# Dense graph layer: front and back products dealt in sixteen equal shares between the builds

## The reference, cut to what matters

```python
ew = _inv_sqrt(out_deg)[row] * w * _inv_sqrt(in_deg)[col]
mf = (x @ W_f.T)[row] * ew[:, None]
y_forward = jax.ops.segment_sum(mf, col, num_segments=n_nodes)
mb = (x @ W_b.T)[col] * ew[:, None]
y_backward = jax.ops.segment_sum(mb, row, num_segments=n_nodes)
y = jnp.concatenate([y_forward, y_backward], axis=-1) + bias_param
```

## Time and profile before

| | us |
|---|---|
| median of 3 runs | 5378.27 |
| lowest and highest run | 5376.85, 5378.61 |
| span of the profiled execution | 5371.9 |
| of it `gnn_dense`, from the first build to the last front sum | 3303.2 to 4639.3 |

### The profile page before, as it was taken

One profiled execution on the slowest core, in us unless ns is written; L12 is line 12 of the kernel. 1 busy time (PEld: TensorE's weight loads), 2 busy tenths in 40 slices (PEclk: granted clock), 3 DMA queues, 4 the chain that ended last, 5 costly groups with the idle time before them and its releaser, 6 DMA issues. The chain is left out here.

```text
span 5371.9 us, 86748 instructions
## 1 busy us (share of the span) xinstructions
PE 4172.9 (78%) x27330; PEld 3017.8 (56%) x27331; DVE 3413.4 (64%) x7289; ACT 1663.0 (31%) x2903; POOL 2167.4 (40%) x2194
## 2 busy tenths in 40 slices
PE   3477777777777777746999945999999999769992
PEld 2355555555555555534888833666656666458872
DVE  6466666666666666687555577888888888640115
ACT  1233333333333333321222264333333333121121
POOL 1477777777777777700666600000000000202220
PEclk9678777777777887756999966999999999759996
DMA  4766666666666666651566543444444444323333
GB/s 122 189 168 170 167 165 170 170 162 170 170 165 167 170 169 163 158 207 68 193 200 199 183 139 84 81 85 89 81 81 88 87 81 85 88 86 121 100 118 103
DMA packets 946866, 733.83 MB, mean 137 GB/s; under 512 B 703102, under 2 KB 832054, under 8 KB 944599
## 3 DMA queue, kind: packets, MB, share of 16 engines
q1 hardware_dynamic: 835851, 433.62, 31.3%
q0 software_dynamic: 104144, 289.95, 20.0%
q10 hardware_dynamic: 6652, 7.32, 0.4%
HBM read 483.39 MB, written 92.34 MB: 107 GB/s over the span
## 5 line engine op out<-in xcount | busy, mean ns | idle before, releaser
L1288 POOL DMA_INDIRECT gat_rows<-h_rows,gat_sources x1664 | 1577.0, 948 | 509.2 <-issue 485.5
L1526 PE MATMUL gat_sum_ps<-gat_rows,gat_onehot 128*128 128x265 f32 x3328 | 1167.6, 510 | 3.2 <-DVE gat_rows L1418 2.4
L1526 PEld LDWEIGHTS gat_sum_ps<-gat_rows,gat_onehot 128*128 128x128 f32 x3328 | 792.9, 250 | 190.4 <-issue 5.7
L2055 ACT CAST gnn_z<-build_ps 128x392 bf16<-128x392 f32 x992 | 473.4, 486 | 847.7 <-PE build_ps L2070 842.3
L1997 DVE TENSOR_TENSOR onehot_low<-dense_codes,dense_iota_bf 128x2048 bf16<-128x2048 bf16 x496 | 604.0, 1218 | 2.6 <-PE build_ps L2070 2.6
L2080 PE MATMUL back_ps<-zb_pieces,gnn_z 128*128 128x384 bf16 x3038 | 567.1, 327 | 0.0
L2102 PE MATMUL front_ps<-x_res_wide,front_rows 128*128 128x448 bf16 x2604 | 562.5, 353 | 0.0
L1976 POOL DMA_INDIRECT front_rows<-zf_piece_rows,vrow_nodes x62 | 64.8, 1046 | 1231.2 <-PE front_ps L2102 1221.0
L1418 DVE TENSOR_TENSOR gat_rows<-gat_rows,gat_numerators_ps 128x1024 f32<-128x1024 f32 x416 | 502.0, 1207 | 0.0
L2471 PE MATMUL moe_hidden_ps<-moe_rows_T,moe_w 128*128 128x256 f32 (+1 forms) x1408 | 459.9, 483 | 2.7 <-DVE moe_rows_T L2512 0.8
L2070 PEld LDWEIGHTS build_ps<-onehot_high,onehot_low 128*128 128x128 bf16 x7936 | 339.4, 98 | 204.6 <-issue 38.5
(11 more groups left out here) (366 smaller groups left out, 5160.4 us busy)
## 6 DMA issues: line engine op xcount, KB each, us to landing
moe_w<-in_L_ffn_W SPq DMA_DIRECT2D x112, 512.0 KB
gat_targets<-gat_step_targets SPq DMA_DIRECT2D x104, 512.0 KB
moe_w<-in_L_ffn_w SPq DMA_DIRECT2D x32, 1024.0 KB
gat_rows<-h_rows,gat_sources POOLq DMA_INDIRECT x1664
moe_rows_out<-moe_slot_zeros SPq DMA_DIRECT2D x36, 512.0 KB
gat_flags<-gat_tile_flags SPq DMA_DIRECT2D x104, 128.0 KB
normal_rows<-moe_xn_all SPq DMA_DIRECT2D x14, 896.0 KB
mid_taken<-moe_rows_out SPq DMA_DIRECT2D x14, 896.0 KB, 7.3
```

The lines of the kernel that those rows point to most:

```text
L1288: pool.indirect_dma_start(out=g[:, b, t, :], out_offset=None, in_=T.h[:, :], in_offset=bass.IndirectOffsetOnAxis(ap=idx[:, b, t:t + 1], ax ...
L1526: last = pe.matmul(po[:, s % BANKS, 0:W], o[:, b, s * SUB + t, :], g[:, b, s * SUB + t, :], start=t == 0, stop=t == SUB - 1)
L2055: nc.scalar.copy(AT[:, k % 2, :, CHUNK * c:CHUNK * (c + 1)], pb[:, c % 2, 0:CHUNK * NT].rearrange("p (u h) -> p h u", u=CHUNK)).then_inc(a ...
```

## The change

The front and back products of a slot are put in one list `run`: for each of seven groups first the 6 front products, then the 7 back products, 91 in all. The list is cut in sixteen shares of 5 or 6, and share c is issued behind the build of chunk c, now also in the chunks 0 and 15. `back_ps` has two banks, used in turn, so TensorE's wait for the sum of the superstep before the last (`q - 2` where it was `q - 1`) replaces that for the last one. The merge moves from chunk 1 to chunk 4. On VectorE the sums follow: a front sum stands four chunks behind the chunk in which its group ends (chunks 1, 3, 5, 7, 10, 12, 14), the sum of the back products behind chunk 15 and so at chunk 3 of the next slot, and the addition of the merged rows at chunk 8. The number of instructions of every kind stays the same.

```diff
+    TERMS = 6
+    MERGE = 4
+    run = [("front", g, n) if n < TERMS else ("back", g, n - TERMS) for g in range(GROUP) for n in range(TERMS + GROUP)]
+    share = [run[c * len(run) // NC:(c + 1) * len(run) // NC] for c in range(NC)]
+    front_done = [[g for kind, g, n in share[c] if kind == "front" and n == TERMS - 1] for c in range(NC)]
...
-        py = k.ps(ctx, "back_ps", [P, 512])
+        py = k.ps(ctx, "back_ps", [P, 2, 512])
...
             def sums(q, k, c):
-                if c == 1 and 2 <= k <= NQ + 1:
+                if c == MERGE and 2 <= k <= NQ + 1:
                     add_back(q, k)
-                if c % 2 and c <= 2 * HALF - 1 and 3 <= k <= NQ + 2:
-                    add_front(q, k, c)
-                if c == 2 * HALF and 1 <= k <= NQ:
+                if 3 <= k <= NQ + 2:
+                    for g in front_done[c]:
+                        add_front(q, k, g)
+                if c == NC - 1 and 1 <= k <= NQ:
                     sum_back(q, k)
...
-            def back(q, k, g):
-                if g == 0:
+            def back(q, k, g, n):
+                h = g * GROUP + n
+                if h == 0:
                     pe.wait_ge(ae, q * NC)
-                    until(pe, yr, q - 1)
...
+                    until(pe, yr, q - 2)
...
             def slot(q, r, k):
                 for c in range(NC):
                     if k < NQ:
                         build(q, k, c)
-                    if c % 2 == 0 and c and 1 <= k <= NQ:
-                        back(q, k, c // 2 - 1)
-                    if c == 1 and 2 <= k <= NQ + 1:
+                    for kind, g, n in share[c]:
+                        if kind == "front" and 3 <= k <= NQ + 2:
+                            front(q, r, k, g, n)
+                        if kind == "back" and 1 <= k <= NQ:
+                            back(q, k, g, n)
+                    if c == MERGE and 2 <= k <= NQ + 1:
                         merge(q, k)
-                    if c % 2 and c <= 2 * HALF - 1 and 3 <= k <= NQ + 2:
-                        front(q, r, k, c)
```

More of the change, by code:

```diff
@@ L1891, in gnn_dense @@
     HALF = PARTS // 2
+    TERMS = 6
[3 more added lines that the diff above has]
+    front_done = [[g for kind, g, n in share[c] if kind == "front" and n == TERMS - 1] for c in range(NC)]
+    assert HALF == GROUP
     io = k.sem("dense_iota")
@@ L1938, in supersteps, with front_at @@
                 slot(q, q // BODY, q)
-        def front_at(k, c):
+        def front_at(k, g):
             first = k % 2
-            return (c - 1) // 2 + (0 if first else HALF), (k - 3 if first else k - 4) % SLOTS
+            return g + (0 if first else HALF), (k - 3 if first else k - 4) % SLOTS
         @block.sync
@@ L2001, in onehots, with add_front @@
                 last.then_inc(oh, 1)
[L2003 to L2006, removed]
+            def add_front(q, k, g):
+                f = q * HALF + (g - 3 * HALF)
+                n = (k * HALF + g - 3 * HALF) % 2
+                at = front_at(k, g)[0] * CN
                 dve.wait_ge(yf, f + 1)
@@ L2015, in sum_back @@
                 dve.tensor_scalar(mrg[:, n, :], i2[:, :], C.vlocal[:, bass.ds(q - 1, 1)], None, ALU.is_equal)
-                dve.tensor_reduce(ybv[:, n, :], py[:, 0:3 * P].rearrange("p (s f) -> p f s", s=3), AX.X,
+                dve.tensor_reduce(ybv[:, n, :], py[:, n, 0:3 * P].rearrange("p (s f) -> p f s", s=3), AX.X,
                                   ALU.add).then_inc(yr, 1)
@@ L2072, in build @@
                 last.then_inc(bu, 1)
-            def back(q, k, g):
-                if g == 0:
+            def back(q, k, g, n):
+                h = g * GROUP + n
+                if h == 0:
                     pe.wait_ge(ae, q * NC)
-                    until(pe, yr, q - 1)
[L2078 to L2083, removed]
+                    until(pe, yr, q - 2)
+                ins = pe.matmul(py[:, (k - 1) % 2, 0:3 * P], AT[:, (k - 1) % 2, h, :], zb3[:, h, :, :].rearrange("p s f -> p (s f)"),
+                                start=h == 0, stop=h == NT - 1)
+                if h == NT - 1:
+                    ins.then_inc(yb, 1)
             def merge(q, k):
@@ L2091, in merge, with front @@
                 last.then_inc(mg, 1)
-            def front(q, r, k, c):
-                if c == 1 and k % 2:
+            def front(q, r, k, g, n):
+                if g == 0 and n == 0 and k % 2:
                     pe.wait_ge(te, q * 16 - 16)
                     pe.wait_ge(zg[0 if k % BODY == 3 else 1], r * 32 + (32 if k % BODY == 3 else 0))
[L2097 to L2105, removed]
+                chunk, first = front_at(k, g)
+                bank = (k * HALF + g - 3 * HALF) % 2
+                if n == 0:
+                    until(pe, ya, q * HALF + (g - 3 * HALF - 1))
+                s, m = n // 3, n % 3
+                ins = pe.matmul(pf[:, bank, 0:CN], zfv[:, first + s, m * P:(m + 1) * P],
+                                AV[:, first + s, chunk * CN:(chunk + 1) * CN], start=n == 0, stop=n == TERMS - 1)
+                if n == TERMS - 1:
+                    ins.then_inc(yf, 1)
             def slot(q, r, k):
```

## The result

| | before | after |
|---|---|---|
| median of 4 runs, us | 5378.44 | 5283.86 |
| lowest and highest, us | 5376.85, 5379.71 | 5281.89, 5287.59 |
| span of the profiled execution, us | 5371.9 | 5283.7 |
| first build to start of the last front sum, us | 1335.5 | 1240.2 |
| distance of two merges, us | 21.23 in the mean | 19.76 |

The ratio is 0.9823, with a 95% interval of 0.9810 to 0.9837: the changed kernel is 94.6 us faster, 1.8%. Forecast were 82 us and a time of 5296 us between 5284 and 5318. The direction and the mechanism came out as forecast; the gain was 13 us larger, and the median lies 0.14 us under the range, with two of the four runs inside it. In a second comparison both kernels were some 7 us faster (5371.3 and 5277.6 us), at the same ratio, 0.9823 (0.9807 to 0.9839).

The account below looks back on a forecast made before the run. TensorE's stream was taken to bound the kernel. 58 slots at 1.36 us (79), 0.7 at the loop's turn and 2 for slots 62 and 63 gave 82 us off 5378, so 5296 us; 8 in 10 range 5284 to 5318.

Parts of the forecast that it names:

- the mechanism: At each slot's end, TensorE's waits for VectorE's back sum and ScalarE's copy go, 1.36 us a slot; forecast 80%.

## What to carry to other kernels

Where one engine's stream bounds a loop, deal its independent work evenly between the steps that hand over to others: here that kept the copies from being outrun, and with it in place neither the second bank nor the later merge, taken back by itself, cost anything in the middle of the layer. Count an instruction's cost by what will stand ahead of it: an fp32 product pair cost 0.09 us more behind short products than behind long ones, and 0.11 more where its weight load had to wait. When a change removes idle time, put the slow stretches that follow such idle into the optimistic end of the range.

## What the runs showed of the hardware that was not expected

A clearing on POOL stops a cast on VectorE altogether: 0.29 us became 10.75 us beside POOL's 5.42 and 5.31. The Trainium skill has the rule, page "SBUF — State Buffer", section "Who interferes with whom": VectorE in some of its modes, which a cast can enter, and GpSimd share a pair of ports, and whoever comes second waits until the other's instruction is over. The trace agrees, and shows that the wait outlasted the first clearing and took in the second. The comparison of the earlier trace rows took 0.54 us in the 29 slots of the kernel before in which it began while a gather of POOL ran, and 0.35 in its 33 others. In the changed kernel it takes 0.35 to 0.36 us in all 62 slots: in 29 of them a gather runs beside it too, but starts 0.03 us behind it.

The clock at the loop's turn fell in some traces and not in others, at idle times of 1.8 to 2.4 us that don't sort the two. The slow products cost 1.8 us in the run with one bank against the changed kernel's turn (the two slots there take 43.26 us for 41.50).
